# Mixture-of-experts layer on one core: the float32 router product with its operands swapped

## The reference

```
y   = clip(((x * styles) @ weight.T) * dcoefs + bias, -256, 256)    # styles, dcoefs per sample
sh  = silu(y @ sh_gate_w) * (y @ sh_up_w) @ sh_down_w               # shared expert, width 1024
s   = sigmoid(y @ router_w.T)                                       # 64 experts
    # of s + e_bias: 8 groups of 8, the best 4 groups by their two best, then the best 8 experts
out = x + sh + sum over a token's 8 experts of w * expert(y)        # width 256 each
```

## Time and profile before

| what | value |
|---|---|
| runs | 4451.37, 4456.83, 4459.96 us |
| the profiled execution: its span, first to last instruction | 4399.4 us |
| median of the runs less that span | 57.4 us |
| PE busy (matmuls) / weight loads | 4019.9 us, 91% / 3273.9 us, 74% |
| DVE / ACT / POOL busy | 1640.3 / 1424.1 / 1959.6 us |
| mean granted clock of PE | 0.947 |

### The profile page before, as it was taken

How to read it: one execution, slowest core, us unless ns; L and a number is a source line. 1 busy time by engine, 2 the same in 40 slices (tenths; PEclk the granted TensorE clock), 3 DMA queues, 4 the chain that set the end, 5 groups by cost and what they waited for, 6 DMA issues and landing times.

```text
span 4399.4 us, 90773 instructions
## 1 busy us (share of the span) xinstructions
PE 4019.9 (91%) x19474; PEld 3273.9 (74%) x19475; DVE 1640.3 (37%) x3485; ACT 1424.1 (32%) x2790; POOL 1959.6 (45%) x1598
## 2 busy tenths in 40 slices
PE   7888988888888886999999999999889999999997
PEld 6766776676676674788878888787668888888886
DVE  4444444444444444333333333333433333333332
ACT  3222222222222221334343344343543343444333
POOL 1232333233343323555555555555455555555554
PEclk8888988898898898999999999999999999999998
DMA  4111111111111111566666666666866666666665
GB/s 161 39 39 38 38 43 38 38 43 39 43 43 38 38 38 35 109 111 124 111 134 113 111 123 128 126 119 125 207 146 116 124 120 115 122 126 122 113 110 105
DMA packets 372915, 408.33 MB, mean 93 GB/s; under 512 B 192457, under 2 KB 227409, under 8 KB 372881
## 3 DMA queue, kind: packets, MB, share of 16 engines
q0 software_dynamic: 135872, 280.60, 35.4%
q1 hardware_dynamic: 237010, 127.35, 11.5%
HBM read 228.83 MB, written 178.93 MB: 93 GB/s over the span
## 4 chain that ended last, share of the span: by engine, by line
PE 27%; DMA 16%; SPq 9%; issue 7%; POOLq 0%; DVE 0%; DVEq 0%; ACT 0%; POOL 0%; ACTq 0%
PE bank L1056 16%; DMA out_dram<-o_rows,list_s 9%; PE bank L1074 8%; SPq L903 6%; DMA list_g<-slot_list 4%; SPq L938 2%; DMA raw_d<-in_L_ffn_down_w_dram 2%; PE bank L1047 2%; PE bank L1065 1%; SPq L955 1%; DMA raw_gu<-in_L_ffn_up_w_dram 0%; POOLq L903 0%; DVE w_dn_l L30 0%; DMA list_s<-slot_list 0%; SPq L957 0%
## 5 line engine op out<-in xcount | busy, mean ns | idle before, releaser
L1009 POOL DMA_INDIRECT out_dram<-o_rows,list_s x532 | 866.6, 1629 | 743.6 <-DMA list_g<-slot_list 370.9
L396 POOL DMA_INDIRECT slot_list<-ent,pos x512 | 522.1, 1020 | 1150.5 <-DVE ent L738 983.3
L1056 PE MATMUL bank<-w_gu_h,x_h 128*128 x2128 | 885.4, 416 | 43.2 <-DVE w_dn_l L30 43.2
L1056 PE MATMUL bank<-w_gu_h,x_l 128*128 x2128 | 844.2, 397 | 0.0
L1056 PE MATMUL bank<-w_gu_l,x_h 128*128 x2128 | 832.6, 391 | 0.0
L993 POOL DMA_INDIRECT x_rows<-y_rows,list_g x536 | 551.8, 1030 | 510.3 <-issue 311.6
L1213 DVE TENSOR_TENSOR e_hf<-bank,e_sg 128x256 f32<-128x256 f32 x532 | 225.6, 424 | 1081.4 <-ACT e_sg L1123 638.0
L30 DVE TENSOR_TENSOR x_l<-bank,x_h 128x512 fp32r<-128x512 f32 x533 | 368.0, 690 | 651.3 <-ACT x_h L1117 407.2
L1117 ACT CAST x_h<-bank 128x512 fp32r<-128x512 f32 x533 | 313.1, 587 | 631.6 <-PE bank L1047 572.0
L1056 PEld LDWEIGHTS bank<-w_gu_h,x_h 128*128 128x128 f32 x2128 | 400.8, 188 | 113.0 <-issue 46.9
L1123 ACT ACTIVATE e_sg<-bank 128x256 f32<-128x256 f32 x532 | 203.9, 383 | 838.2 <-PE bank L1056 794.8
(11 more groups left out here) (196 smaller groups left out, 5985.0 us busy)
## 6 DMA issues: line engine op xcount, KB each, us to landing
xin<-in_x_dram SPq DMA_DIRECT2D x16, 1024.0 KB
y_rows<-yrow SPq DMA_DIRECT2D x64, 256.0 KB
stage_d<-in_x_dram SPq DMA_DIRECT2D x16, 1024.0 KB
out_dram<-stage_d SPq DMA_DIRECT2D x16, 1024.0 KB
raw_gu<-in_L_ffn_gate_w_dram SPq DMA_DIRECT2D x29, 512.0 KB
raw_gu<-in_L_ffn_up_w_dram SPq DMA_DIRECT2D x29, 512.0 KB
raw_d<-in_L_ffn_down_w_dram SPq DMA_DIRECT2D x29, 512.0 KB
list_g<-slot_list SPq DMA_DIRECT2D x536, 1.0 KB
```

The costliest lines, as they stand in the source:

```text
L396: nc.gpsimd.indirect_dma_start(slots, bass.IndirectOffsetOnAxis(ap=pos[:, t, k:k + 1], axis=0), ent[:, t, k, :], None).then_inc(scattered, 16)
L1009: nc.gpsimd.indirect_dma_start(out, bass.IndirectOffsetOnAxis(ap=ls[u][:, 0:1].bitcast(U32), axis=0), og[u][:], None, compute_op=ALU.add). ...
L1056: last = nc.tensor.matmul(b_gu[u % 2][:], xp[a][:, u % 2, k, :], wgu[b][:, bass.ds(place, 1), k, :].rearrange("p a n -> p (a n)"), start=( ...
```

## The change

The router product swaps its operands: for each of the 4 feature groups the 64 columns of `rt` are loaded and all 512 columns of `yt` stream, so one accumulation of 4 matmuls gives the logits with experts on the partitions. ACT copies them to `lt`, PE turns them back in 4 transposes (`turn_logits`), and the sigmoid reads these. In body, route stands between up(7) and down(6), turn_logits between down(6) and down(7).

`xt` and `yp` become one pair of buffers, `cols`, of which there are two: block q's x columns are overwritten by its y columns, and the next block takes the other pair. y_high and y_low move into chunk 5. The loops of PE, ACT and DVE run over two bodies at a time. `wn` takes the space of `sbi`. The pieces of `routing` are spread anew, and in chunks 3 and 4 they stand ahead of the clips:

```diff
-            xt = [sb("xt_h", [P, KC, TB], F32R), sb("xt_l", [P, KC, TB], F32R)]
+            cols = [[sb(f"cols{n}_h", [P, KC, TB], F32R), sb(f"cols{n}_l", [P, KC, TB], F32R)] for n in range(2)]
-            yp = [sb("y_h", [P, KC, TB], F32R), sb("y_l", [P, KC, TB], F32R)]
+            lt = sb("lt", [E, TB])
-            wn = sb("wn", [P, TT, E])
+            wn = sbi
...
                 def turn_x(q, k, first):
                         if not first:
-                            if some(TT * q):
-                                pe.wait_ge(act_yrow, TT * q)
+                            pe.wait_ge(act_sc, q)
                     elif k == 1:
                         if not first:
-                            if some(q):
-                                pe.wait_ge(act_sc, q)
+                            pe.wait_ge(act_lt, q)
...
                 def route(q):
                     pe.wait_ge(act_yrow, TT * q + 3)
+                    for k in range(KC):
+                        last = nc.tensor.matmul(misc[1][0:E, :], rt[:, k, :], yt[:, k, :], start=(k == 0), stop=(k == KC - 1))
+                    last.then_inc(pe_lt, 1)
+
+                def turn_logits(q):
+                    pe.wait_ge(act_yrow, TT * q + TT)
+                    pe.wait_ge(act_lt, q + 1)
+                    pe.nop(nofuse=True)
                     for t in range(TT):
-                        for k in range(KC):
-                            last = nc.tensor.matmul(misc[1][:, t * E:(t + 1) * E], yt[:, k, t * P:(t + 1) * P], rt[:, k, :],
-                                                    start=(k == 0), stop=(k == KC - 1))
+                        last = nc.tensor.transpose(misc[0][:, t * E:(t + 1) * E], lt[:, t * P:(t + 1) * P], ident[0:E, 0:E])
                     last.then_inc(pe_lg, 1)
...
-                def body(i, prep):
+                def body(i, prep, v):
-                        if c == (3 if prep else 2):
+                        if c == 3:
                             ranks(i, prep)
+                        if prep and c == NCH - 1:
+                            route(i + 1)
                         if c:
                             down(i, c - 1)
...
-                        if prep and c == 7:
-                            route(i + 1)
+                        if prep and c == NCH - 1:
+                            turn_logits(i + 1)
                     down(i, NCH - 1)
...
-                with pe.Fori(1, NBLK - 1) as i:
-                    body(i, True)
-                body(NBLK - 1, False)
+                with pe.Fori(0, NBLK // 2 - 1) as g:
+                    body(2 * g + 1, True, 1)
+                    body(2 * g + 2, True, 0)
+                body(NBLK - 1, False, 1)
...
-                def x_high(q, k):
+                def x_high(q, k, v):
-                        if some(KC * q):
-                            act.wait_ge(pe_y, KC * q)
+                        if some(NCH * (q - 1)):
+                            act.wait_ge(pe_u, NCH * (q - 1))
...
-                def y_high(q):
+                def y_high(q, v):
                     act.wait_ge(dve_y, KC * (q + 1))
-                    if some(NCH * q):
-                        act.wait_ge(pe_u, NCH * q)
+                    act.wait_ge(pe_y, KC * (q + 1))
                     for k in range(KC):
-                        nc.scalar.copy(yp[0][:, k, :], yt[:, k, :]).then_inc(act_yh, 1)
+                        nc.scalar.copy(cols[v][0][:, k, :], yt[:, k, :]).then_inc(act_yh, 1)
+
+                def logits_out(q):
+                    act.wait_ge(pe_lt, q + 1)
+                    if some(q):
+                        act.wait_ge(pe_lg, q)
+                    nc.scalar.copy(lt[:], misc[1][0:E, :]).then_inc(act_lt, 1)
...
+                        if prep and c == 5:
+                            y_high(i + 1, 1 - v)
...
                     if prep:
-                        y_high(i + 1)
+                        logits_out(i + 1)
                         scores(i + 1)
...
-                pieces_of = {0: 2, 1: 1, 3: 1, 4: 1, 5: 2, 6: 2}
-                pieces_of_last = {0: 3, 2: 2, 3: 2, 4: 2}
+                pieces_of = {0: 1, 1: 1, 2: 1, 3: 1, 4: 2, 5: 1, 6: 2}
+                pieces_of_last = {0: 2, 1: 1, 3: 3, 4: 3}
...
-                        if prep and c == 3:
-                            next(pieces)
+                        if prep and c == 5:
+                            y_low(i + 1, 1 - v)
+                        for _ in range((pieces_of if prep else pieces_of_last).get(c, 0)):
+                            next(pieces, None)
                         if prep and c in (3, 4):
                             y_clip(i + 1, 2 * (c - 3))
                             y_clip(i + 1, 2 * (c - 3) + 1)
-                        if prep and c == NCH - 1:
-                            y_low(i + 1)
-                        if not prep or c != 3:
-                            for _ in range((pieces_of if prep else pieces_of_last).get(c, 0)):
-                                next(pieces, None)
```

More of the change, by code:

```diff
@@ L324, in build @@
             act_yh, dve_yl = sem("act_yh"), sem("dve_yl")
-            pe_lg, act_sc, dve_sc = sem("pe_lg"), sem("act_sc"), sem("dve_sc")
+            pe_lt, act_lt, pe_lg = sem("pe_lt"), sem("act_lt"), sem("pe_lg")
+            act_sc, dve_sc = sem("act_sc"), sem("dve_sc")
             pe_g, act_sg, pe_u, dve_h = sem("pe_g"), sem("act_sg"), sem("pe_u"), sem("dve_h")
@@ L435, in turn_x, with make_y @@
                     last.then_inc(pe_tx, 1)
-                def make_y(q, m, first):
+                def make_y(q, m, first, v):
+                    xt = cols[v]
                     if m == 0:
@@ L470, in ranks @@
                     else:
-                        pe.wait_ge(act_yrow, TT * NBLK)
+                        pe.wait_ge(act_sc, NBLK)
                     pe.wait_ge(dve_mask, i + 1)
@@ L477, in ranks, with gate @@
                     last.then_inc(pe_rank, 1)
-                def gate(i, c):
+                def gate(i, c, yp):
                     if c == 0:
@@ L528, in _ @@
                 for m in range(KC):
-                    make_y(0, m, True)
+                    make_y(0, m, True, 0)
                 for t in range(TT):
@@ L574, in scores @@
                         act.wait_ge(dve_sc, q)
-                    nc.scalar.activation(sc[:].rearrange("p t e -> p (t e)"), misc[1][:, 0:TT * E], ACT.Sigmoid).then_inc(act_sc, 1)
+                    nc.scalar.activation(sc[:].rearrange("p t e -> p (t e)"), misc[0][:, 0:TT * E], ACT.Sigmoid).then_inc(act_sc, 1)
                 def gate(i, c):
@@ L602, in body @@
                     if prep:
-                        y_high(i + 1)
+                        logits_out(i + 1)
                         scores(i + 1)
                 for k in range(KC):
-                    x_high(0, k)
+                    x_high(0, k, 0)
                 for m in range(KC):
                     y_scale(0, m)
+                y_high(0, 0)
                 for t in range(TT):
                     y_row(0, t)
-                y_high(0)
+                logits_out(0)
                 scores(0)
-                body(0, True)
-                with act.Fori(1, NBLK - 1) as i:
-                    body(i, True)
-                body(NBLK - 1, False)
+                body(0, True, 0)
+                with act.Fori(0, NBLK // 2 - 1) as g:
+                    body(2 * g + 1, True, 1)
+                    body(2 * g + 2, True, 0)
+                body(NBLK - 1, False, 1)
             STEPS = 20 + 3 * TT + 5 * TT
@@ L636, in y_clip, with y_low @@
                     nc.vector.tensor_scalar(yt[:, m, :], yt[:, m, :], CLAMP, -CLAMP, ALU.min, ALU.max).then_inc(dve_y, 1)
-                def y_low(q):
+                def y_low(q, v):
                     for k in range(KC):
                         dve.wait_ge(act_yh, KC * q + k + 1)
-                        sub_exact(nc, yp[1][:, k, :], yt[:, k, :], yp[0][:, k, :]).then_inc(dve_yl, 1)
+                        sub_exact(nc, cols[v][1][:, k, :], yt[:, k, :], cols[v][0][:, k, :]).then_inc(dve_yl, 1)
                 def hidden(i, c):
@@ L845, in _ @@
                 for k in range(KC):
-                    x_low(0, k)
+                    x_low(0, k, 0)
                 for m in range(KC):
                     y_clip(0, m)
-                y_low(0)
-                body(0, True)
-                with dve.Fori(1, NBLK - 1) as i:
-                    body(i, True)
-                body(NBLK - 1, False)
+                y_low(0, 0)
+                body(0, True, 0)
+                with dve.Fori(0, NBLK // 2 - 1) as g:
+                    body(2 * g + 1, True, 1)
+                    body(2 * g + 2, True, 0)
+                body(NBLK - 1, False, 1)
         dense.close()
```

33 lines of the change are left out of this document (17 added, 16 removed).

## The result

The changed kernel takes **4347.6 us** (median of 4 runs, 4346.5 to 4349.9) against 4456.1 for the kernel before (4 runs, 4451.4 to 4460.0): ratio 0.976, interval 0.974 to 0.977. The two profiles show only half of it: their spans are 4399.4 and 4344.8 us, 54.6 apart. The rest lies between the profiled execution of the kernel before and its runs, and no trace shows it. A second surprise came with the first experiments: the gain depends on the chip. On two other chips the changed kernel was faster again (0.982, 0.984), on a third it was slower (1.007).

What follows compares the result with a forecast made beforehand. A block was taken as 84 to 85 us of matmuls plus a scatter-time window passing only some 20 records. The terms -31 + 3 + 5 + 5 = -18 gave span 4381.6, time 4439 us; range 4385 to 4485.

Steps and rivals of the forecast that it cites:

- step 2: Slow window beside the scatters: starting them 7.3 us earlier changes its content, -2.0 us a block, -31 with step 1.
- Rival (b): DVE's last entries piece comes late, POOL's scatters pause after the 24th, other engines recover; -148 us, 4291; chance 0.13.
- Step 1: Router product: 8 float32 records and four transposes replace 32 records; -0.3 us a block, between -2.1 and +4.8.
- Step 3: ACT's y_high and DVE's y_low move into chunk 5: nothing in blocks, +3 us in the prologue, ends 0 and 5.
- step 5: Last body: scatters start a chunk later, so the window outlasts PE's remaining work; +5 us, ends 0 and 8.
- Step 4: Logits copy and new waits: PE's down(6), 2.8 us, covers the about 0.6 us that ACT needs; costs nothing.
- Step 6: Two-body loops of PE, ACT and DVE may need instruction fetches at 6 jumps back; +5 us, 0 to 15.
- rival (c): The double loop is fetched anew at each turn: 27 us in place of 5, 4461; chance 0.12.
- (a): Late ACT and DVE answers fall on chunk 6, PE's up of chunk 7 waits; +65 us, 4504; chance 0.17.
- (d): The window costs the same whatever PE does in it; step 2 falls to 0, +26 us, 4465; chance 0.13.
- The sum's base: Sum made against the profiled span, 4399.4 us; the 57.4 up to the runs' median, 4456.8, carried over.
- The range's upper end: 4485 us, reached by (d) and rival (c) together, 26 + 22.

Runs made afterwards that it cites:

- The product alone: Kernel before with only the swapped product, its copy, transposes and waits: 4374.8 us against 4415.9 on a trickling chip (before over 4400 us), ratio 0.989.
- the pieces alone: Kernel before with both DVE entries pieces of chunk 4 ahead of the clips, one in chunk 5: 4329.6 us against 4410.5 (trickling), 4062.7 against 4069.1 (calm).
- two bodies alone: Kernel before with only the loops of PE, ACT and DVE over two bodies: 4414.2 us against 4415.9 on a trickling chip, ratio 1.000.
- The kernels with groups: Trickling chips: kernel before with a block's 32 scatters in four groups 4098.5 us (0.930), in two 4254.0 (0.964); changed kernel with four 4130.5 (0.934).

## Why the prediction was wrong

It said faster, 4439, by 18 us; it is 108 on that chip (54.6 by the two profiles), 76 and 75 on two others. Its picture of what bounds the kernel held in every run: matmuls of 84 to 85 us and a window that belongs to the stretch of scatters. **The step that failed is step 2**: it let the window slide with its length kept, and took a full stretch of 32 scatters for granted. Measured in block 4, the window is 16.6 us and not 22.6, because POOL stops for 10.4 us behind the 24th scatter; PE's idle time over blocks 0 to 14 fell from 225 to 166 us. The window's content was wrong too: it was to begin 22.3 us after the first scatter with up and the product of chunk 7, and began at 17.7 with down products and y's transposes, 14 records in place of 20. Rival (b) described what happened, a late last piece, a pause behind the 24th scatter and the others' recovery, and was given 0.13, although the prediction had itself read that DVE came 4.5 us late in the earlier trace rows. The reason against it, that DVE's chains aren't slowed where they need no other engine, was true and beside the point: the piece stands in DVE's queue behind the product of chunk 6, which does need PE and ACT, and DVE stood still for 18.9 us before that one. The size of (b) was off as well. It took 11.4 us a block from the two short periods of the earlier trace rows, where the pause comes after 17 and 19 scatters; the new one comes after 24, when PE has already trickled for 13 us. The periods fell by some 5 us (106.9 to 102).

- **Step 1, the product, -0.3 a block.** On a calm chip +0.9. The new records were priced well (3.58 us against 3.7), the old ones not: they take 3.49 in a block, at full clock, against the prologue's 4.34, where the granted clock was 0.82; and the seams weren't in it. The Trainium skill (FP8 and Floating Point Precision, TensorE Precision Notes) has four passes for true FP32; by it the new product takes 16 passes of 0.23 us, an estimate of 3.7, and the trace agrees with 3.58. For the old one four passes of its 1,024 columns would be 1.8 us, and the trace has 3.49.
- **Step 2's content of the window, -31.** The product alone gave 41 on a trickling chip, so the direction was right, but hardly by the content: by the rows above the window was shorter where the copy came in time, and as long as before where it didn't. In the change nothing of it shows, as the pieces alone gave as much as the whole (81 against 75). The two gains, 41 and 81, don't add.
- **Step 3, prologue +3, and step 5, last body +5.** The first was 2.1. Both together are -1 on the calm chips (the dense stage's 19.8 less 20.7).
- **Step 4, nothing.** Right for 13 of the 15 blocks; in blocks 7 and 14 the transposes stood 12.2 and 16.9 us before ACT's copy, inside the slow stretch, in place of a trickle. In the product-alone kernel the same wait took up to 23.3 us of a block. The cover of 2.8 us was sized for an ACT that issues at once.
- **Step 6, +5, and rival (c).** The fetches are real: 57 packets on q14, some at every turn of the loop, with two stalls beside them on the calm chip, 8.5 us, and nothing that two bodies alone showed on a trickling one. The rule of the Trainium skill that was cited (Runtime: NRT & Kernel Launch, Instruction fetch mechanics) left open whether PE's loop stays in its store. If q8 is PE's queue, which no row says, the answer differs: 16 packets against 13 on the calm chips, 25 and 34 against 14 on the trickling ones, where a part of them stands in the middle of the loop.
- **Rivals (a) and (d)** are out. (a) was right that the late answers would fall on chunk 6 (DVE's product came 18 us late there), but PE's up of chunk 7 never waited for it, since PE was slow itself. (d) had the periods unmoved.
- **The sum's base.** 57.4 us around the span don't exist; the changed kernel's first profile has 1.7. The profiled execution was 55 us faster than the runs beside it, so the sum started from another base than the time that it was held against. The range's upper end, by its own terms (26 + 22), would be 4487 and not 4485.

## What to carry to other kernels

When a trace shows an engine issuing slowly without a wait, ask what another engine does at that time without pause, and test by spacing that work out before tuning what happens to lie in the slow stretch; here a few lines of waits were worth 312 us, and the redesigned product showed no gain where the stretch was broken. Follow each engine's queue order into the slow stretch: a piece of work that needs nobody is late if what stands ahead of it needs somebody. And measure a change beside its base on more than one chip, because this program's time differed by 8 to 10% between chips, and the change's sign with it.

## What the runs showed of the hardware

- A stretch of indirect scatters from POOL, one every 1.26 to 1.6 us, slows the issue of ACT and DVE from 11 to 14 us after its start and of PE from 18 to 24 us (12 to 14 in a short stretch that follows others closely), until 2 to 3 us after its end, on some chips; on others the same stretch slows nothing (117 records of PE in place of 22 in a window of 22.6 us). Pauses of 4 to 9 us between stretches of 10 us prevent it.
- Why the chips differ is open. One number goes with it: the ten traces from trickling chips (the first pair's among them) hold 34,700 to 37,400 records of semaphore updates, the ten from calm ones 54,000 to 54,400. The kernels with groups on trickling chips are among the first ten though they hardly trickle, so missing records don't by themselves go with slowness. "Remote" stands only in traces from trickling chips, where the releaser's record is missing. The Trainium skill (NOTIFIC — the notification-queue block, 7.1) says that the block that carries such records can hold back the engines that produce them. That would fit a stretch with many updates (an argument, since no row counts them in the stretch), and would mean that the slowness comes with the recording; no run here takes the recording away, so this is a guess.
- A loop over two bodies of the code of PE, ACT and DVE brings instruction packets at every turn, one over a single body doesn't: 57 packets against 19 on the queue q14.
